# A graph network's gather stage: a semaphore raised by a drain of TensorE in place of the last matmul of four steps

## The reference

```python
transformed = jnp.einsum('ni,rio->rno', h, weight)
msg = transformed[rel_type, src] * norm
out = jax.ops.segment_sum(msg, dst, num_segments=h.shape[0])
```

## Time and profile before

| what | value |
|---|---|
| runs | 3165.93, 3170.58, 3170.78 us; median 3170.58 |
| span of the profiled execution (first to last instruction) | 3179.1 us |
| busy in that span: PE, PEld, DVE, ACT, POOL | 1968.0 (62%), 1556.4 (49%), 1545.2 (49%), 927.1 (29%), 1402.9 us (44%) |
| gather stage, from POOL's first gather to DVE's last add | 315.3 to 896.1 us |

### The profile page before, as it was taken

The page is one execution under the profiler, slowest core; times in us unless marked ns, Lnnn a source line. Parts: engine busy times, 40 slices in busy tenths (PEclk is TensorE's granted clock), DMA queues, the critical chain, the costliest instruction groups (busy, mean ns, idle before and its releaser), DMA issues.

```text
span 3179.1 us, 37685 instructions
## 1 busy us (share of the span) xinstructions
PE 1968.0 (62%) x10259; PEld 1556.4 (49%) x10259; DVE 1545.2 (49%) x4920; ACT 927.1 (29%) x2035; POOL 1402.9 (44%) x1415
## 2 busy tenths in 40 slices
PE   7998344353367999734555564564365455555599
PEld 6887233243237999623443343443244344344377
DVE  4200133233276555634564564575365555566853
ACT  4443576673013444320111111113011111111432
POOL 1000666666603443245555555513555555553143
PEclk9999676666678999876776766787576776677799
DMA  6444565554238999743344344323333443442000
GB/s 215 187 199 192 171 210 187 193 196 141 87 88 279 353 355 351 240 149 117 104 127 124 100 130 124 100 69 104 109 120 117 117 120 116 119 122 88 1 14 28
DMA packets 207421, 473.85 MB, mean 149 GB/s; under 512 B 33230, under 2 KB 100370, under 8 KB 200750
## 3 DMA queue, kind: packets, MB, share of 16 engines
q0 software_dynamic: 63520, 179.35, 20.0%
q1 hardware_dynamic: 112878, 190.07, 16.7%
q10 hardware_dynamic: 30816, 101.99, 9.0%
HBM read 367.19 MB, written 104.90 MB: 148 GB/s over the span
## 4 chain that ended last, share of the span: by engine, by line
another core or an unknown queue 29%; PE 29%; DVE 27%; issue 10%; DVEq 3%; POOL 1%; DMA 1%; ACT 1%; SPq 0%; POOLq 0%; ACTq 0%
PE banks L421 9%; PE banks L1256 7%; DVE arena L1661 3%; DVE arena L1745 3%; PE banks L1268 3%; DVE arena L825 3%; DVE X L834 2%; DVE arena L1710 2%; DVEq L696 2%; DVEq L699 1%; PE banks L1422 1%; DVE xn L1673 1%; POOL arena L1463 1%; PE banks L2164 1%
## 5 line engine op out<-in xcount | busy, mean ns | idle before, releaser
L1463 POOL DMA_INDIRECT arena<-ht,srcT x784 | 783.7, 1000 | 696.7 <-DVE arena L1745 400.8
L783 POOL DMA_INDIRECT arena<-tr,idx1T x392 | 376.5, 961 | 398.3 <-DMA tr<-arena 207.9
L1572 PE MATMUL banks<-arena,XT 128*128 128x264 f32 x884 | 392.6, 536 | 229.1 <-DVE arena L1745 148.5
L811 PE MATMUL banks<-arena 128*128 x884 | 257.1, 454 | 327.0 <-DVE arena L825 258.1
L811 PEld LDWEIGHTS banks<-arena 128*128 128x128 f32 x884 | 196.2, 229 | 388.0 <-issue 356.1
L1572 PEld LDWEIGHTS banks<-arena,XT 128*128 128x128 f32 x884 | 213.2, 260 | 296.8 <-DVE arena L1745 158.5
L1573 PE MATMUL banks<-arena,XT 128*128 128x264 f32 x884 | 358.0, 496 | 0.0
L1745 DVE TENSOR_TENSOR arena<-arena,nrmT 128x528 f32<-128x528 f32 x442 | 309.9, 703 | 20.8 <-ACT nrmT L1519 12.4
L834 DVE TENSOR_TENSOR X<-X,banks 128x256 f32 x221 | 92.6, 419 | 395.3 <-remote 367.6
L421 PE MATMUL banks<-parts 128*128 128x512 f32 x1200 | 275.1, 391 | 4.7 <-DVE parts L381 4.7
L1573 PEld LDWEIGHTS banks<-arena,XT 128*128 128x128 f32 x884 | 228.5, 259 | 58.8
(11 more groups left out here) (366 smaller groups left out, 3284.0 us busy)
## 6 DMA issues: line engine op xcount, KB each, us to landing
arena<-in_L_ffn_w_dram SPq DMA_DIRECT2D x195, 512.0 KB
tr<-arena SPq DMA_DIRECT2D x50, 1024.0 KB, 3.9
XT<-otd ACTq DMA_DIRECT2D x52, 512.0 KB
arena<-ohd ACTq DMA_DIRECT2D x52, 512.0 KB
arena<-dld ACTq DMA_DIRECT2D x28, 512.0 KB
otd<-arena ACTq DMA_DIRECT2D x28, 512.0 KB
ohd<-arena ACTq DMA_DIRECT2D x28, 512.0 KB
arena<-ht,srcT POOLq DMA_INDIRECT x784
```

What stands on the lines that cost most here:

```text
L783: pool.indirect_dma_start(Gr[:, o:o + D], None, TR, bass.IndirectOffsetOnAxis(ap=idx1T[:, q:q + 1], axis=0)).then_inc(d_g[b % NG], 16)
L811: mm = ten.matmul(B[n][:, 0:D], OHr[:, n, h, :], Gr[:, h * D:][:, bass.ds(o, D)], start=(h == 0), stop=(h == 1))
L1463: pool.indirect_dma_start(Gall[:, o:o + ROW], None, HT[L], bass.IndirectOffsetOnAxis(ap=srcT[:, q:q + 1], axis=0)).then_inc(d_g[b % NG], 16)
L1572: ten.matmul(B[n][:, 0:MSG], OH[b][:, 2 * j, :], WG[:, j, 0, :], start=True, stop=False)
```

## The change

In `pe_gather` the last matmul of four steps no longer carries the increment. Behind it PE executes a drain, which waits until PE's earlier instructions are through, and the drain raises gm_ok. What gm_ok counts, who waits for it and at which values stays the same.

```diff
                 for h in range(2):
                     o = ten.snap(rp[k][i], min_val=0, max_val=(RB - 1) * 2 * D)
-                    mm = ten.matmul(B[n][:, 0:D], OHr[:, n, h, :], Gr[:, h * D:][:, bass.ds(o, D)], start=(h == 0), stop=(h == 1))
+                    ten.matmul(B[n][:, 0:D], OHr[:, n, h, :], Gr[:, h * D:][:, bass.ds(o, D)], start=(h == 0), stop=(h == 1))
                 if s % GS == GS - 1 or s == SU - 1:
-                    mm.then_inc(gm_ok, 1)
+                    ten.drain().then_inc(gm_ok, 1)
```

## The result

The changed kernel takes 3201.5 us (median of 4 runs, 3191.8 to 3204.0), the kernel before 3170.7 us (4 runs, 3165.9 to 3171.8): 30.8 us more, ratio 1.010, interval 1.0085 to 1.0114. The forecast was 3160.6 us, the range 3105 to 3190: wrong in sign and outside the range. What came is rival B's shorter rounds, and a longer tail that B had not priced; B's own figure was 3188.3 us, "up to 3200" if the first signal behind a release comes late too.

The account below looks back on a forecast made before the run. The prediction took POOL's gathers, with 74.5 us of waits, to set the gather stage's end. Fewer waits (-11.5 us) and the tail's drains (+1.5) made -10 us off 3170.58: 3160.6 us, range 3105 to 3190.

Parts of the forecast that it names:

- rival B: Gather stage: the drain is held like the matmul's signal and rounds get shorter; 3188.3 us, up to 3200; chance 0.30.
- The reading of the timeline: Gather stage: the signal DVE takes belongs to matmuls ended 18.9 us earlier or more, held until POOL stops issuing.
- Rival D: Gather stage: signals were never late, something else released DVE; only the tail's 1.5 us change, 3172 us; chance 0.09.
- The price of B for shorter rounds: POOL's waits: rounds of 8 blocks instead of 12, 24.5 waits of 3.7 us, 90.7 us in all, +16.2 us.
- the drain's signal comes through within a few us: Late in a round: PE's instructions still advance, some 1.4 us each, so the drain's signal isn't held long.
- the longer rounds: POOL's rounds grow to 16 to 20 blocks; 11 waits of 5.7 us instead of 16 waits, -11.5 us.
- the drain's own cost: On PE: 28 us for 56 drains, hidden in PE's waits except for three drains in the tail, +1.5 us.
- The bubble: On PE behind each drain: the drain and the restart of the next matmul, 0.5 us together.
- 13 steps: Tail behind POOL's last gather: some 13 steps are left, holding three drains.
- the restart: PE's first matmul behind a drain starts cold: 0.79 us at most against 0.379, 0.41 us more.
- two at a time for a larger part of each round: Sign in the profile after: PE's matmuls come in pairs for more of each round if the forecast is right.
- The slow stretch: Late in a round, from about 10 us behind POOL's restart: PE gets on slowly, at 4.8 us a step.

Follow-up runs that it names:

- x6: The changed kernel with a 256-column memset ahead of each POOL gather, so gathers start 1.56 us apart: 3250.4 us, ratio 1.0145 to the kernel before.
- x7: The kernel before with a 256-column memset and its wait ahead of each POOL gather, so gathers start 1.56 us apart: 3245.6 us, ratio 1.0129.
- x1: The changed kernel with gm_ok raised again by each group's last matmul and a drain without a signal behind it: 3228.4 us, ratio 1.0115 to the kernel before.
- x5: The kernel before with POOL allowed 36 blocks ahead of gm_ok in place of 20: 3208.6 us, ratio 1.0054.
- x13: The kernel before with a 32-column memset and its wait ahead of each POOL gather: 1.99% slower than the kernel before, which took 2684.0 us.
- z1: x13 run a third time, beside a kernel before that took 3168.1 us: 3159.0 us, ratio 0.9976.
- x8: The kernel before with only the first of each step's two PE matmuls: 3190.3 us, ratio 0.9962.
- x9: The kernel before with POOL allowed 12 blocks ahead (NEAR = 12) instead of 20: ratio 0.9999, where the kernel before took 2684.0 us.
- y1: The changed kernel once more, beside a kernel before that took 2684.8 us: 2681.7 us, ratio 0.9993.
- y3: x9 once more, beside a kernel before that took 2684.8 us: ratio 1.0002.
- the paced kernels: The kernel before or the changed one with a memset ahead of each or each second POOL gather: 2.35%, 2.16% and 1.99% slower in their first job.

## Why the prediction was wrong

**What held.** The reading of the timeline: the signal that releases DVE and POOL is long overdue, and in 15 of the 18 "remote" waits of the kernel before it comes 2.9 to 4.0 us behind POOL's last gather. One of the other three ends at 359.98, while POOL gathers, 18.2 us behind its matmul, so POOL's pause is not the whole rule. x6 and x7 show that the density of the gathers matters, which was only inferred there. Rival D, and with it the rule of the Trainium skill (TensorE: Matmul & The Clock Gate, "The cost: per-tile semaphore tail": by its formula, for one tile and one increment, an estimate of 25 + 4.7 + 26.3 = 56 ns behind the last matmul), falls for this stage: 11.7 us for the drain shown above. Where nothing is held the trace is close to it: in x7 each waiting add starts some 0.04 us behind the last matmul's end, which is itself modelled. The price of B for shorter rounds, +16.2 us, came as +14.7, with POOL's wait of 3.48 to 3.51 us in the rounds of eight blocks shown (3.70 in the short rounds of before). That it came so close is in part luck: there were 22 waits and not 24.5, and two of them lasted 9.6 and 11.8 us.

**The step that failed** is this one: "I take it that the drain's signal comes through within a few us." It rested on PE's matmuls and ACT's activations, which late in a round still start, 1.4 us apart. That an engine's instructions start doesn't tell when the drain behind them ends. x1 shows it alone: the drain stands for 4.9 us in the median and up to 30, with no signal of its own to send. With that the working of the longer rounds (n = 21, 11 waits, -11.5 us) has nothing to stand on.

**The term that was mis-sized**: the drain's own cost, "+1.5 us" in the tail, measured +17.7. The bubble was right (0.43 us; I took 0.5), the rest of the term was missing. PE's first two groups of the tail, with the granted clock behind the busy times:

```profile
901.00:908.00 7.00, 6.65 (x16) 5.06 (x16) 2.06 (x9) 0.00 (x0) 0.00 (x0) 0.56 0.00 0
908.00:912.00 4.00, 3.72 (x16) 2.96 (x16) 3.35 (x12) 0.00 (x0) 0.00 (x0) 1.00 0.01 2
```

- The tail doesn't keep its 13 steps: a drain held while POOL finishes leaves 21, 8.5 more at 3.72/4 = 0.93 us, 7.9 us.
- PE starts only at 901.18, 3.0 us behind POOL's last gather: 1.3 us until the held drain ends, 1.7 for two register loads and the bubble. I had listed PE's waits behind the drain, but not the loads of each eighth step.
- The first group takes 6.65 us instead of 3.72, 2.9 more. PE had idled for 12.2 us, and the granted clock was 0.56 in this stretch, mostly the lower level (1.2 GHz), and 1.00 in the next. I had priced the restart as one slow matmul, 0.41 us.
- Five more bubbles are 2.2 us, and two more pairs of loads, at 1.3 us each, 2.6.

These make 18.6 us; the last adds end 1.2 us behind PE's last matmul and not 2.0, which leaves 17.8. Rival B had priced the tail at the same 1.5 us and so gave 3188.3, 13 us short.

**A sign that went the other way.** I expected PE's matmuls "two at a time for a larger part of each round". The slow stretch has gone instead, and the signals are late all the same. The register instruction that PE executes once a step, in the kernel before and in the changed one:

```profile
L804 PEldq ALU_OP  x221: 4/33/1409, 312.8 to 891.1; - x111
```

```profile
L804 PEldq ALU_OP  x221: 32/33/42, 314.0 to 927.1; - x111
```

Late in a round of before it lasts 0.70 us; in the changed kernel PE stands in a drain at that time, and no such instruction is slow. So the slow stretch was no measure of how soon a drain would come through.

**Chances.** B had 0.30, less than the forecast's 0.36, on no better ground than that one step. x5 also corrects a belief of mine about the rounds: more room doesn't lengthen them.

## What to carry to other kernels

A drain ties an engine's next instructions to the ends of all earlier ones (in the changed kernel the next matmul starts 0.41 us behind the drain's end or later), so where ends become known late, it turns a late signal into an idle engine; ask of a moved signal not only who waits for it but what the new carrier itself must wait for. Count what stands behind it on its engine, register loads included, and look where the stage ends: steps that a late signal leaves over run uncovered, and cost as much here as the waits added in its middle (17.7 and 14.7 us). When two engines are released together by something that the profile can't name, slow down or thin out the third one in an experiment before building on a guess.

## What the runs showed of the hardware

- The signals of PE's matmuls, and the ends of PE's drains, can be known many microseconds late while POOL issues indirect gathers 1.26 us apart: 12 to 25 us behind the recorded end of the matmul in the rounds of the kernel before, 46 at most; 4.6 to 34.9 us for 24 drains of the changed kernel. At the pace of x13 (1.40 us where nothing is held) this is still so for part of the time (z1), at 1.56 us it is gone (x6, x7). With half of PE's matmuls the lateness is smaller (x8), for a reason that stays open.
- With gathers 1.26 us apart most of the held signals come 1 to 4 us after POOL pauses (before, changed kernel, x1), but not all: in x8 14 of 28, and in z1 22 of 25, come while it gathers.
- After 12.2 us of idle time PE's next 16 matmul records took 6.65 us at a granted clock of 0.56, and the 16 behind them 3.72 us at 1.00.
- The same kernel took 3168 to 3205 us in four jobs and 2684 us in two others, with the 15 and 21 runs of a job within 0.5%. In the traces of the latter (x9, y1, y3 and the paced kernels; the kernel before has none there) nothing was held: the gather stage's POOL time is 494.6 us in x9, not 567, and the two attention stages, which also gather with indirect DMAs, take 510 to 515 us each from first to last gather, not 694 to 710. These traces can't tell what differed between the jobs; one chip showed both within eleven minutes. In these runs gathers 1.26 us apart are not enough for a hold: something outside the kernel must come with them. Each execution here was recorded by the profiler, if only for its span and clock, so nor does any run show whether signals are late when nothing is recorded. So a change to a signal in such a stage has to be judged beside the kernel before in the same job, and may cost 1% in one and nothing in another.
- A drain on PE with nothing held (y1) lasts 1.9 us in the median and ends 0.02 us behind the recorded end of the matmul in front of it, so nearly all of it is the matmuls; it leaves PE idle for 0.43 us until the next matmul starts.
